# An LSTM on one core: the gates in two PSUM banks, products of 256 columns, x prepared two steps at a time

## The reference

```python
xW = jnp.einsum('ntd,dk->tnk', x, Wx) + b          # x (32, 512, 512), Wx (512, 2048)
def step(carry, xw_t):
    prev_h, prev_c = carry
    a = xw_t + prev_h @ Wh                          # (32, 2048)
    i = sigmoid(a[:, :H]); f = sigmoid(a[:, H:2*H])
    o = sigmoid(a[:, 2*H:3*H]); g = tanh(a[:, 3*H:])
    next_c = f * prev_c + i * g
    next_h = o * tanh(next_c)
    return ((next_h, next_c), next_h)
out = x + transpose(hs, (1, 0, 2))
```

## Time and profile before

| | us |
|---|---|
| median of 3 runs | 2706.27 |
| lowest, highest | 2705.07, 2707.74 |
| the profiled execution's own time | 2708.34 |
| its span, first to last instruction | 2706.5 |
| PE busy in that span | 2657.2 (98%) |
| weight loads (PEld) busy | 1271.7 (47%) |
| DVE busy | 1440.3 (53%) |
| ACT busy | 868.7 (32%) |

### The profile page before, as it was taken

How to read it: one execution, slowest core, us unless ns; L and a number is a source line. 1 busy time by engine, 2 the same in 40 slices (tenths; PEclk the granted TensorE clock), 3 DMA queues, 4 the chain that set the end, 5 groups by cost and what they waited for, 6 DMA issues and landing times.

```text
span 2706.5 us, 110492 instructions
## 1 busy us (share of the span) xinstructions
PE 2657.2 (98%) x49154; PEld 1271.7 (47%) x49154; DVE 1440.3 (53%) x4642; ACT 868.7 (32%) x2721; POOL 0.2 (0%) x4
## 2 busy tenths in 40 slices
PE   3999999999999999999999999999999999999999
PEld 1444444444444444444444444444444444444445
DVE  4555555555555555555555555555555555555554
ACT  3333333333333333333333333333333333333332
POOL 0000000000000000000000000000000000000000
PEclk8999999999999999999999999999999999999999
DMA  7011011010010110100101101101001011011000
GB/s 161 16 31 31 16 31 30 16 31 23 24 31 16 31 31 16 31 25 22 31 17 29 31 16 31 31 16 31 23 23 31 16 31 31 16 31 28 19 16 17
DMA packets 141588, 76.08 MB, mean 28 GB/s; under 512 B 8837, under 2 KB 140549, under 8 KB 140549
## 3 DMA queue, kind: packets, MB, share of 16 engines
q1 hardware_dynamic: 141440, 75.79, 11.2%
q10 hardware_dynamic: 132, 0.07, 0.0%
HBM read 42.27 MB, written 33.55 MB: 28 GB/s over the span
## 4 chain that ended last, share of the span: by engine, by line
PE 98%; DMA 1%; SPq 1%; DVE 0%; issue 0%; ACT 0%; DVEq 0%; ACTq 0%
PE gates L170 98%; DMA w_raw<-in_L_cond_Wh_dram 1%; SPq L131 1%; DVE w_lo L321 0%; SPq L122 0%; SPq L149 0%; ACT w_hi L248 0%; DVE x_ring L312 0%; ACT i_f L227 0%; ACT tanh_c L234 0%; DVE c_state L290 0%; DVE h_full L296 0%; DVE f_c L286 0%; DVE i_g L288 0%; DVEq L104 0%
## 5 line engine op out<-in xcount | busy, mean ns | idle before, releaser
L170 PE MATMUL gates<-w_hi,xT 128*32 128x512 f16 x16384 | 1060.9, 379 | 25.2 <-ACT gates L218 25.2
L227 ACT ACTIVATE i_f<-gates 128x256 f32<-128x256 f32 x512 | 197.1, 385 | 1527.2 <-PE gates L170 1527.2
L286 DVE TENSOR_TENSOR f_c<-i_f,c_state 128x128 f32<-128x128 f32 x512 | 149.5, 292 | 975.1 <-ACT i_f L227 975.1
L170 PEld LDWEIGHTS gates<-w_hi,xT 128*32 128x32 f16 x16384 | 431.3, 97 | 479.7 <-ACT gates L218 26.1
L170 PE MATMUL gates<-w_hi,hT_hi 128*32 128x512 f16 x8192 | 530.6, 379 | 16.6 <-DVE w_lo L321 16.6
L170 PE MATMUL gates<-w_lo,xT 128*32 128x512 f16 x8192 | 530.8, 379 | 0.0
L170 PE MATMUL gates<-w_lo,hT_hi 128*32 128x512 f16 x8192 | 530.5, 379 | 0.0
L170 PE MATMUL gates<-w_hi,hT_lo 128*32 128x512 f16 x8192 | 529.9, 379 | 0.0
L170 PEld LDWEIGHTS gates<-w_lo,xT 128*32 128x32 f16 x8192 | 215.8, 97 | 227.1 <-issue 0.8
L170 PEld LDWEIGHTS gates<-w_lo,hT_hi 128*32 128x32 f16 x8192 | 215.7, 97 | 227.2 <-issue 1.1
L170 PEld LDWEIGHTS gates<-w_hi,hT_lo 128*32 128x32 f16 x8192 | 215.6, 97 | 226.8 <-issue 0.7
(11 more groups left out here) (19 smaller groups left out, 591.0 us busy)
## 6 DMA issues: line engine op xcount, KB each, us to landing
x_ring<-in_x_dram SPq DMA_DIRECT2D x256, 128.0 KB, 2.8
out_dram<-x_ring SPq DMA_DIRECT2D x252, 128.0 KB, 2.1
w_raw<-in_L_cond_Wx_dram SPq DMA_DIRECT2D x16, 256.0 KB, 10.0
w_raw<-in_L_cond_Wh_dram SPq DMA_DIRECT2D x16, 256.0 KB, 19.6
out_dram<-x_ring SPq DMA_DIRECT2D x8, 64.0 KB, 1.8
bias_raw<-in_L_cond_b_dram SPq DMA_DIRECT2D x4, 64.0 KB, 13.6
h_raw<-in_cond_dram ACTq DMA_DIRECT2D x1, 64.0 KB
```

The lines of the kernel that those rows point to most:

```text
L170: mm = nc.tensor.matmul(gates[bank][j * N:(j + 1) * N, :], stationary, w[:, which, k, j, :], start=False, stop=False, skip_group_check=True)
L227: nc.scalar.activation(i_f[:, :], bank[:, 0:2 * P], ACT.Sigmoid, scale=UNSCALE).then_inc(if_ready, 1)
L286: nc.vector.tensor_tensor(f_c[:, :], i_f[:, P:2 * P], c_state[:, :], ALU.mult)
```

## The change

The gates of a step get two banks: i and f in columns 0 to 255 of one, o and g in columns 0 to 255 of the other. Each matmul of 512 columns becomes two of 256. In `project` and in `recur` the half i,f comes before the half o,g, with one exception: the products with hT_lo of both halves come after all those with hT_hi. `gates_ready` becomes two semaphores. ACT starts i_f on the first and waits for the second ahead of g_gate. The seed writes both banks with one activation. GROUP goes from 4 to 2: casts, splits, transposes and ring additions have 256 columns and come in every second step, both transposes in the same step as x_lo. PE's loop body is four steps (`2 * GROUP`) where the other engines keep eight. The last chunk is stored in four parts where it was two.

```diff
-GROUP = 4
+GROUP = 2
...
-        gates = [psum(f"gates{p}", [P, G], F32) for p in range(2)]
+        gates = [psum(f"gates{p}", [P, 2, G], F32) for p in range(2)]
...
-        gates_ready = sem("gates_ready")
+        half_ready = [sem("if_gates_ready"), sem("og_gates_ready")]
...
-        def steps(engine, step):
+        def steps(engine, step, body=CHUNK):
-            with nc.Fori(0, CHUNKS - 1, engines=(engine,), hint_back_edge=True) as c:
-                for s in range(CHUNK):
-                    step(c, s, CHUNK)
+            with nc.Fori(0, T // body - 1, engines=(engine,), hint_back_edge=True) as c:
+                for s in range(body):
+                    step(c, s, body)
...
-            def add(bank, stationary, w, which, k):
+            def add(bank, half, stationary, w, which, k):
                 for j in range(J):
-                    mm = nc.tensor.matmul(gates[bank][j * N:(j + 1) * N, :], stationary, w[:, which, k, j, :],
+                    mm = nc.tensor.matmul(gates[bank][j * N:(j + 1) * N, half, 0:G // 2], stationary,
+                                          w[:, which, k, j, half * (G // 2):(half + 1) * (G // 2)],
                                           start=False, stop=False, skip_group_check=True)
...
+                for half in range(2):
+                    for part, w in ((0, w_hi), (0, w_lo), (1, w_hi)):
+                        for k in range(J):
+                            add(s % 2, half, xT[:, slot, part, r, k * N:(k + 1) * N], w, 0, k)
...
             def recur(t, s):
                 pe.wait_ge(hT_hi_ready, now)
-                for w in (w_hi, w_lo):
-                    for k in range(J):
-                        add(s % 2, hT_hi[:, k * N:(k + 1) * N], w, 1, k)
-                pe.wait_ge(hT_lo_ready, now)
-                for k in range(J):
-                    mm = add(s % 2, hT_lo[:, k * N:(k + 1) * N], w_hi, 1, k)
-                mm.then_inc(gates_ready, 1)
+                for half in range(2):
+                    for w in (w_hi, w_lo):
+                        for k in range(J):
+                            add(s % 2, half, hT_hi[:, k * N:(k + 1) * N], w, 1, k)
+                pe.wait_ge(hT_lo_ready, now)
+                for half in range(2):
+                    for k in range(J):
+                        mm = add(s % 2, half, hT_lo[:, k * N:(k + 1) * N], w_hi, 1, k)
+                    mm.then_inc(half_ready[half], 1)
...
-                act.wait_ge(gates_ready, t + 1)
+                act.wait_ge(half_ready[0], t + 1)
...
+                act.wait_ge(half_ready[1], t + 1)
-                nc.scalar.activation(g_gate[:, :], bank[:, 3 * P:4 * P], ACT.Tanh,
+                nc.scalar.activation(g_gate[:, :], bank[:, 1, P:2 * P], ACT.Tanh,
...
                     if r == 0:
                         split_x(group + 1)
-                    if r == 1:
                         transpose_x(0, slot)
-                    if r == 2:
-                        dve.wait_ge(x_lo_ready, t + (GROUP + GROUP - r))
+                        dve.wait_ge(x_lo_ready, t + 2 * GROUP)
                         transpose_x(1, slot).then_inc(xT_ready, GROUP)
```

More of the change, by code:

```diff
@@ L26, in lstm_residual @@
     CHUNKS = T // CHUNK
-    assert T % CHUNK == 0 and CHUNK == 2 * GROUP and CHUNKS > SLOTS
+    assert T % CHUNK == 0 and CHUNK == 4 * GROUP and CHUNKS > SLOTS
     X_DMA = 16 * J
@@ L100, in lstm_residual @@
         block = ctx.enter_context(nc.Block())
-        def steps(engine, step):
-            with nc.Fori(0, CHUNKS - 1, engines=(engine,), hint_back_edge=True) as c:
-                for s in range(CHUNK):
-                    step(c, s, CHUNK)
-            for s in range(CHUNK):
-                step(CHUNKS - 1, s, CHUNK - 1 - s)
+        def steps(engine, step, body=CHUNK):
+            with nc.Fori(0, T // body - 1, engines=(engine,), hint_back_edge=True) as c:
+                for s in range(body):
+                    step(c, s, body)
+            for s in range(body):
+                step(T // body - 1, s, body - 1 - s)
         def ring_of(group):
@@ L162, in _, with project @@
                 store((CHUNKS - 1) % SLOTS, T - CHUNK, first, GROUP)
-            sp.wait_ge(out_stored, (CHUNKS + 1) * X_DMA)
+            sp.wait_ge(out_stored, (CHUNKS - 1 + CHUNK // GROUP) * X_DMA)
         @block.tensor
         def _(pe):
-            def add(bank, stationary, w, which, k):
+            def add(bank, half, stationary, w, which, k):
                 for j in range(J):
-                    mm = nc.tensor.matmul(gates[bank][j * N:(j + 1) * N, :], stationary, w[:, which, k, j, :],
+                    mm = nc.tensor.matmul(gates[bank][j * N:(j + 1) * N, half, 0:G // 2], stationary,
+                                          w[:, which, k, j, half * (G // 2):(half + 1) * (G // 2)],
                                           start=False, stop=False, skip_group_check=True)
                 return mm
-            def project(t, s, waits=False):
+            def project(s, waits=False):
                 slot, r = (s // GROUP) % 2, s % GROUP
-                for part, w in ((0, w_hi), (0, w_lo), (1, w_hi)):
-                    for k in range(J):
[L178 to L182, removed]
+                for half in range(2):
+                    for part, w in ((0, w_hi), (0, w_lo), (1, w_hi)):
+                        for k in range(J):
+                            if waits and not half:
+                                pe.wait_ge(w_lo_ready if w is w_lo else w_hi_ready, k + 1)
+                            add(s % 2, half, xT[:, slot, part, r, k * N:(k + 1) * N], w, 0, k)
             def recur(t, s):
@@ L186, in recur @@
                 pe.wait_ge(hT_hi_ready, now)
-                for w in (w_hi, w_lo):
-                    for k in range(J):
-                        add(s % 2, hT_hi[:, k * N:(k + 1) * N], w, 1, k)
-                pe.wait_ge(hT_lo_ready, now)
-                for k in range(J):
-                    mm = add(s % 2, hT_lo[:, k * N:(k + 1) * N], w_hi, 1, k)
-                mm.then_inc(gates_ready, 1)
+                for half in range(2):
[4 more added lines that the diff above has]
+                for half in range(2):
+                    for k in range(J):
+                        mm = add(s % 2, half, hT_lo[:, k * N:(k + 1) * N], w_hi, 1, k)
+                    mm.then_inc(half_ready[half], 1)
             def step(c, s, left):
-                t = c * CHUNK + s
+                t = c * (2 * GROUP) + s
                 recur(t, s)
@@ L201, in step @@
                     pe.wait_ge(seeded, t + 2)
-                    project(t + 1, (s + 1) % CHUNK)
+                    project((s + 1) % (2 * GROUP))
             pe.wait_ge(zeros_ready, 1)
             for p in range(2):
-                mm = nc.tensor.matmul(gates[p][:, :], zeros[:, 0:P], zeros[:, :], start=True, stop=True)
+                for half in range(2):
+                    mm = nc.tensor.matmul(gates[p][:, half, :], zeros[:, 0:P], zeros[:, :], start=True, stop=True)
             mm.then_inc(banks_open, 1)
@@ L209, in _ @@
             pe.wait_ge(xT_ready, GROUP)
[L210 to L213, removed]
+            project(0, waits=True)
+            pe.wait_ge(w_lo_ready, 2 * J)
+            steps(mybir.EngineType.PE, step, 2 * GROUP)
         @block.scalar
@@ L217, in seed @@
             def seed(t, s):
-                nc.scalar.activation(gates[s % 2][:, :], bias_raw[:, :], ACT.Copy, scale=WSCALE).then_inc(seeded, 1)
+                nc.scalar.activation(gates[s % 2][:, :, 0:G // 2], bias_raw[:, :].rearrange("p (b m) -> p b m", b=2),
+                                     ACT.Copy, scale=WSCALE).then_inc(seeded, 1)
             def cast_x(group):
@@ L224, in step @@
                 t = c * CHUNK + s
-                act.wait_ge(gates_ready, t + 1)
+                act.wait_ge(half_ready[0], t + 1)
                 bank = gates[s % 2]
-                nc.scalar.activation(i_f[:, :], bank[:, 0:2 * P], ACT.Sigmoid,
+                nc.scalar.activation(i_f[:, :], bank[:, 0, 0:2 * P], ACT.Sigmoid,
                                      scale=UNSCALE).then_inc(if_ready, 1)
-                nc.scalar.activation(g_gate[:, :], bank[:, 3 * P:4 * P], ACT.Tanh,
+                act.wait_ge(half_ready[1], t + 1)
+                nc.scalar.activation(g_gate[:, :], bank[:, 1, P:2 * P], ACT.Tanh,
                                      scale=UNSCALE).then_inc(g_ready, 1)
-                nc.scalar.activation(o_gate[:, :], bank[:, 2 * P:3 * P], ACT.Sigmoid,
+                nc.scalar.activation(o_gate[:, :], bank[:, 1, 0:P], ACT.Sigmoid,
                                      scale=UNSCALE).then_inc(o_ready, 1)
@@ L240, in step @@
                         act.wait_ge(x_loaded, (t + (GROUP + CHUNK)) * (X_DMA // CHUNK))
-                    cast_x(c * 2 + (s // GROUP + 1))
+                    cast_x(c * (CHUNK // GROUP) + (s // GROUP + 1))
             def split_hi(n):
@@ L281, in step @@
             def step(c, s, left):
```

(2 more changed lines are left out.)

## The result

The changed kernel takes 2737.16 us (median of 4 runs, 2735.83 to 2738.06), the kernel before 2706.51 us. The ratio is 1.0111, with a 95% interval of 1.0099 to 1.0123: slower by 30.7 us, 1.1%. The profiled execution took 2737.91 us, its span is 2736.1 us.

What follows compares the result with a forecast made beforehand. PE's gapless product stream was taken as the bound, with the recurrent chain just hidden. Products +30.7, loop exit +1.0 and ends -0.8 gave +30.9 us on the 2706.3 us median: 2737 us, range 2703 to 2785.

Steps and rivals of the forecast that it cites:

- the loop's exit: Where PE's loop ends: instructions come late once, queued work lasts half as long, so the stall grows by 1.0 us.
- Products: PE's stream: 12268 more quartets (four column products of one k) at a fixed 2.5 ns each, +30.7 us.
- The step left open: In each quartet: whether the 2.5 ns belong to the product (+30.7 us) or go with its columns (0).
- Instructions and weight loads at no cost: PE's stream: a load-product pair every 27.3 ns is delivered, and loads stay hidden under 256-column products; cost zero.
- Rivals 2 and 3: Each quartet: weight load gets too little cover, about 2782 us, 12%; or instructions arrive too slowly, near 3000 us, 10%.
- rival 3: PE's instruction delivery: sustained rate too slow, +265 us at 30 ns a pair, nearly double at 54; 10%, back edge included.
- Loops: PE's loop: 127 back edges instead of 63 cost zero; the stall at the exit grows by 1.0 us.
- The part of rival 3 on the back edge: PE's loop: a back edge longer than the 0.87 us queued work covers, at most +109 us; within the 10%.
- The chain: Recurrent chain to the new h: slack grows from 0.06 to about 0.33 us; PE was not waiting, gain zero.
- x two steps at a time: DVE and ACT preparing x every second step: all hidden, DVE with 0.8 us spare before its next f_c.
- Ends: Behind the last product: shorter chain, last add and last store, -0.8 us.
- The start: Start of the kernel: bound by w_lo, the slow clock stays; change zero.

Runs made afterwards that it cites:

- e9: The changed kernel with products of 128 columns, PE's loop body two steps and x prepared two steps ahead; 2899.4 us, ratio 1.0713 to the kernel before.
- e4: Kernel before with GROUP = 2, PE's body four steps and a second, useless weight load ahead of each 512-column product; 2704.80 us, ratio 0.9992.
- e10: Kernel before with GROUP = 2, PE's body four steps and only the h products 256 columns wide, one bank; 2721.61 us, ratio 1.0054.
- e2: Kernel before with GROUP = 2 and all products of 256 columns, but all gates in one bank; 2737.81 us, ratio 1.0113.
- e12: e9 with products of 256 columns in place of 128, PE's body still two steps; 2737.07 us, ratio 1.0111 to the kernel before.
- e1: Kernel before with only GROUP = 2 (x prepared two steps at a time), products still 512 columns in one bank; 2705.88 us, ratio 0.9992.
- e5: Kernel before with h_full computed ahead of h_hi, one more DVE operation in the chain; 2785.54 us, ratio 1.0291.
- e7: Changed kernel with h_full ahead of h_hi and a useless o_gate by tanh_c product before it; 2746.73 us, ratio 1.0140 to the kernel before.

## Why the prediction was right

The time (2737 forecast, 2737.16 measured) and the mechanism that makes nearly all of it hold. A smaller term, the loop's exit, has the right size for a reason that the runs do not bear out; that part of the agreement is luck. Term by term:

- **Products: +30.7 us.** Right. From the hT_lo products of step 1 (56.07) to those of step 508, the first behind the loop (2712.76), the change has 507 steps of 5.240 us, 109.17 ns a quartet, 2.50 over the columns; e9 has 2.5 at 128 columns. The step left open, that the price belongs to the product, is shown by e4 and e10. A step was 5.180 us before, so 511 steps x 0.0598 = 30.6 us.
- **Instructions and weight loads at no cost.** Right, for 256 columns: 14 ns a pair and 55.8 ns a quartet still run (e9). Rivals 2 and 3 fall. The floor of about 25 ns from start to start that rival 3 quotes from the Trainium skill ("TensorE: Matmul & The Clock Gate", section "Wait — 56ns, not 53.3ns?") does not hold here across the four column tiles: e9 has a product every 14 ns.
- **Loops: back edges 0, exit +1.0 us.** The back edges are right. The exit is right in size: the last three steps are 0.19, 0.58 and 0.24 us too long, 1.0 us in all against 0.09 before. But the reason given, that the queued work lasts half as long, is not borne out. e2 has the same loop and products of the same length on PE and no stall there (5.24 us to its last step, rows below), nor has e12; e1, with PE's stream of the kernel before, has 0.42 us. What sets these stalls stays open, and the agreement is luck. The part of rival 3 on the back edge was a real mechanism with the wrong width: it sets in between 256 and 128 columns.
- **The chain: slack 0.06 before, 0.33 after, no gain.** The 0.06 is borne out (e5). The 0.33 was 0.39 (e7). g starts 0.34 after the last quartet's start, not 0.37; the prediction let ACT start 0.48 behind it before the change, where its own rows give 0.43 (1000.64 to 1001.07). The rest of the chain is 0.03 shorter. The slack did not enter the time.
- **x two steps at a time: hidden.** Right. DVE's three operations run from 1008.39 to 1009.50 and its next f_c starts at 1010.85, 1.35 us to spare where 0.8 was forecast; e1 has no loss.
- **Ends: -0.8 us.** From the last h quartet to the end it is 5.85 us (2730.25 to 2736.1) against 6.73, so -0.9.
- **The start: 0.** In the profiled execution it was -1.3 us: step 1's x products start at 51.59 and not at 52.91, since the weights landed sooner (17.7 us from issue to landing against 19.6, the median of the loads of Wh) and the low clock took a part of it back. The span grew by 29.6 us: 31.7 between step 1's x products and the last hT_lo products (30.6, the exit and a rest of the low clock), -1.3 ahead of them and -0.8 behind their start. This is a difference of executions; the medians differ by 30.7.

Here are the exit's first stall in the PE timeline of the changed kernel (0.62 us where four calls of `add` take 0.44), and the last add, which answers to the earlier trace rows. Between them stand the same two places of e2, where the last steps are 5.24 us:

```profile
2717.57 0.89 PE L171 MATMUL gates<-w_lo,hT_hi 128*32 128x256 f16 x16
2718.19 1.14 PE L171 MATMUL gates<-w_hi,hT_lo 128*32 128x256 f16 x32
...
2729.49 1.14 PE L171 MATMUL gates<-w_hi,hT_lo 128*32 128x256 f16 x32
```

```profile
2722.20 1.04 PE L171 MATMUL gates<-w_hi,hT_lo 128*32 128x256 f16 x32
...
2727.44 1.06 PE L171 MATMUL gates<-w_hi,hT_lo 128*32 128x256 f16 x32
```

```profile
2732.38 0.42 DVE L315 TENSOR_TENSOR x_ring<-x_ring,h_full 128x256 f32<-128x256 f32 x1
```

## What to carry to other kernels

When the timeline shows an engine streaming without a gap, overlapping the others with it better gives nothing; count instead what each of its instructions pays besides its data, and keep products as wide as the bank allows. Before a change shortens or lengthens a chain, read its slack: the start of the load that needs its result against the moment at which the stream would run dry, and test it by one operation of known length. And when instructions get shorter and more, look at the loop too: its body's size and the work queued at its back edge.

## What the hardware showed that I had not expected

- The price of a product at the full clock is the same 2.5 ns at 512, 256 and 128 columns, for four tiles together; a second weight load per product costs nothing.
- A loop body of 3072 loads and products is fetched anew every round (13.60 MB of instructions), one of 1536 is not (0.20 MB); where between the two this begins was not tried.
- A back edge costs PE 0.32 us with products of 128 columns and nothing with 256.
- The stall at a loop's exit varied between kernels with the same PE stream or nearly so: 0.09 us in the kernel before and 0.42 in e1, 1.0 in the change and none in e2.
